# Writing out the order of all fourteen tile pairs of a fused cross-attention and sign-weight layer, and moving sums from VectorE to ScalarE

## The chip, the cores and the metric

One core of a Trainium2 chip runs the whole program. The metric is the device time in microseconds (us). The core has TensorE (PE in the profile; its weight loads are PEld), VectorE (DVE), ScalarE (ACT), GpSimd (POOL) and SyncE (SP), which here only issues DMAs.

## The reference

```python
def _layernorm(x, axis=-1, eps=1e-05):
    m = jnp.mean(x, axis=axis, keepdims=True)
    v = jnp.var(x, axis=axis, keepdims=True)
    return (x - m) / jnp.sqrt(v + eps)

# x (4, 1024, 2048), ctx (4, 64, 2048), weight (2048, 2048), bias (2048,), all float32
def xattn(query, key):
    a = jnp.einsum('bqd,bkd->bqk', query, key)
    e = jax.nn.softmax(a, axis=-1)
    return jnp.einsum('bqk,bkd->bqd', e, key)

def ffn(x, weight_real, bias):
    W = jnp.mean(jnp.abs(W), axis=1, keepdims=True) * jnp.sign(W)   # W = weight_real
    return jnp.einsum('bsi,oi->bso', x, W) + bias

x = x + jnp.tanh(g_xattn[0]) * xattn(_layernorm(x), ctx)
x = x + jnp.tanh(g_ffn[0]) * ffn(_layernorm(x), weight, bias)
```

The `ffn` lines are written here with its inner function opened.

## The kernel before, in words

The 4096 rows of x are 32 tiles of 128 rows, u = 0 to 31; each batch of 8 tiles has its own 64 keys. The work on a tile has two halves.

**Attention.** The first layer norm needs the mean and variance of the tile's rows. Tiles 0 to 2 get them on VectorE (`ln1_mean`, L1144: four `bn_stats` of 512 columns and a `bn_aggr`), the later ones on ScalarE (`sum_rows1` L730, then `square_rows1` L737, which squares x minus the mean; both write out a sum). The constant that divides them is `DVE_LN1`. GpSimd turns these into a scale and a shift of one value per row (`scale1`, `mean_1`, `rstd1`). ScalarE writes the normalised rows (`direct_high_q`, L755) and their float16 high part into `natural`, VectorE the low part (`low_q`, L1169), and a DMA transpose brings them to TensorE (`turn_q`, L411; tile 0 and tile 0 of the second norm are turned by TensorE itself). `scores(u)` (L1842) is 32 matmuls; then VectorE's `max_logits`, ScalarE's `exp`, VectorE's `split_probs` (L1215), TensorE's `transpose_probs` (L1866), ScalarE's `copy_pt` and four `attend(u, n)` (L1871), one for each 512 columns. All four write one PSUM bank, `c_ps`, so `attend(u, n + 1)` waits until VectorE's `attention(u, n)` (L1228) has added the last one to x. `attention` also takes a `bn_stats` of each chunk and a `bn_aggr` after the fourth: these are the second norm's statistics, for all 32 tiles.

**The product with the signs.** GpSimd's `scale2` (L624, four small operations) makes scale and shift, ScalarE's `normalise2` (L772) writes the normalised tile to `xn_a` or `xn_b`. Tiles 0 to 3 are multiplied plainly (`plain_block`, L1882: four quarters of 8 matmuls for each of 16 blocks). Tiles 4 to 31 go in 14 pairs p, each by a scheme of seven products instead of eight: blocks A11, A12, S3, S2, S1, A22, S4, where VectorE makes the S blocks by subtraction and addition (`make_s1` to `make_s4`). Each block goes to `natural` as a high and a low part (`high_a`, `low_a`), is turned by DMA into one of four slots of `ring_a` (`turn_a`, L420), and is multiplied in four `half_product(p, j, n, g)` (L1904) of 8 matmuls. `finish_pair` (L1254) is the VectorE work that combines, scales and adds the results to x; `store(u)` writes the tile out. A11 of pair p needs tile 2p + 5 normalised (`high_a`, L798).

**The weights.** 16 blocks of 128 rows are loaded (`load_w`), their signs written by ScalarE (`sign`, L846), the row sums of |w| taken by ScalarE (`sum_abs`, L854) or, for the blocks in `ABS_DVE` = (2, 5, 8, 11, 14), by VectorE (`sum_abs`, L1322), and the signs turned by TensorE (`turn_w`, L1824) and copied out (`take_w`). TensorE spreads the sums over columns (`turn_alpha`); a product's result is multiplied by them at the end. `make_t1`, `make_t2`, `make_t3`, `make_n4` are eight VectorE additions on the signs that the seven-product scheme needs before pair 0.

**The order of the work.** Every engine has its own program, in order, held together by semaphores. The lists are written out by hand for the start and for pairs 0 and 1. From pair 2 on each engine runs a loop over pairs with three bodies: one for pairs in `KEYS_PERIOD` (2, 6, 10: new keys arrive for the next batch), one for the pair after such a pair, and one regular. In every body f = 2p + 8 is the tile whose scores are next. Two lines of TensorE's program, with no product between them, stand at the end of the body for pairs 3, 7 and 11 (and, as `scores(11)`, at the end of pair 1):

```python
                    scores(f + 1)
                    transpose_probs(f + 1)
```

`NAT`, `REGULAR`, `SWITCH`, `AFTER` list the order in which blocks pass through the three slots of `natural`; `TURNS` the order of TensorE's own transposes.

Of the kernel before, what the change touches and what calls it, by code (L numbers as in the profile page):

```python
# [14 lines left out]
def flamingo_gated_kernel(  # L15
# [56 lines left out]
    TURNS = [("q", 0, 0), ("k", 0, 0), ("k", 0, 1), ("q", 0, 1), ("w", 0, 0), ("w", 1, 0), ("alpha", 0, 0),  # L72
              ("w", 2, 0), ("x1", 0, 0), ("w", 3, 0), ("x1", 0, 1), ("w", 4, 0), ("alpha", 1, 0), ("w", 5, 0),
# [11 lines left out]
    REGULAR = [("S1", 0, 0), ("A22", 0, 0), ("q", 0, 0), ("q", 0, 1), ("S4", 0, 0), ("A11", 1, 0), ("q", 1, 0),  # L85
               ("q", 1, 1), ("A12", 1, 0), ("S3", 1, 0), ("S2", 1, 0)]
    SWITCH = [("S1", 0, 0), ("A22", 0, 0), ("S4", 0, 0), ("q", 0, 0), ("q", 0, 1), ("A11", 1, 0), ("A12", 1, 0),
              ("S3", 1, 0), ("q", 1, 0), ("S2", 1, 0), ("q", 1, 1)]
    AFTER = [("S1", 0, 0), ("q", 0, 0), ("q", 0, 1), ("A22", 0, 0), ("S4", 0, 0), ("q", 1, 0), ("q", 1, 1),
             ("A11", 1, 0), ("S3", 1, 0), ("A12", 1, 0), ("S2", 1, 0)]  # L90
    for p in range(2, PAIRS_N):
# [27 lines left out]
    ABS_DVE = (2, 5, 8, 11, 14)  # L119
# [7 lines left out]
    def seq_y(t, n):  # L127
        return CHUNKS.index((t, n))
# [10 lines left out]
    with ExitStack() as ctx:  # L139
# [38 lines left out]
        sum1 = sb("sum1", [P, 1])  # L178
        mean1 = sb("mean1", [P, 1])
# [123 lines left out]
        mv2_set = sem("mv2_set")  # L303
        ve2_set = sem("ve2_set")
# [53 lines left out]
        DVE_LN1 = 3  # L358
# [6 lines left out]
        def _(sp):  # L365
# [74 lines left out]
            load_w(0)  # L440
            load_gates()
            load_w(1)
            load_x(1)
            load_w(2)
            load_w(3)
            load_w(4)
            load_x(2)
            load_x(3)
            turn_q(1, 0)
            load_w(5)  # L450
            turn_q(1, 1)
            load_w(7)
            load_w(6)
            turn_q(2, 0)
            turn_q(2, 1)
            load_w(8)
            load_bias()
            load_w(9)
            load_x(4)
            turn_x1(1, 0)  # L460
            turn_q(3, 0)
            turn_x1(1, 1)
            load_w(10)
            load_w(11)
            turn_q(3, 1)
            load_w(13)
            turn_x1(2, 0)
            load_w(12)
            turn_x1(2, 1)
            load_w(14)  # L470
            load_w(15)
            turn_q(4, 0)
            load_x(5)
            turn_q(4, 1)
            turn_q(5, 0)
            turn_q(5, 1)
            store(0)
            turn_x1(3, 0)
            load_x(6)
            turn_x1(3, 1)  # L480
            store(1)
            load_keys(1)
            load_x(7)
            turn_q(6, 0)
            store(2)
            turn_q(6, 1)
            load_x(8)
            turn_q(7, 0)
            turn_a(0, "A11")
            turn_q(7, 1)  # L490
            turn_a(0, "A12")
            turn_a(0, "S3")
            turn_a(0, "S2")
            turn_a(0, "S1")
            turn_a(0, "A22")
            store(3)
            turn_a(0, "S4")
            load_x(9)
            turn_q(8, 0)
            turn_q(8, 1)  # L500
            turn_keys(1)
            turn_a(1, "A11")
            store(4)
            turn_a(1, "A12")
            turn_a(1, "S3")
            load_x(10)
            turn_q(9, 0)
# [1799 lines left out]
```

## Time and profile before

| what | value |
|---|---|
| median of 3 runs | 1014.23 us (1010.57 to 1014.42) |
| the profiled execution's own time | 1012.6 us |
| its span, first to last instruction | 1010.8 us |
| busy: PE, DVE, ACT, POOL | 941.6, 870.4, 563.7, 149.8 us |
| mean granted TensorE clock | 0.981 of full speed |

The busy time of PE counts pipelined matmuls with modelled ends; where it is below a stretch's length, PE waited. The idle time of an engine matters where it is the one that sets the end.

### The profile page before, as it was taken

The page shows a single profiled execution, that of the slowest core. Times are in us where ns is not written, and L with a number is a line of the kernel's source. Part 1 is how long each engine was busy: PE and PEld are TensorE (multiplying, and loading weights), DVE is VectorE, ACT ScalarE, POOL GpSimd, SP SyncE. Part 2 cuts the span into 40 slices and gives each one's busy share as a digit, 9 for nine tenths or more (in the row PEclk, how much of TensorE's full clock was granted, in tenths as well). Part 3 has the DMA queues.
Part 4 walks back from the last instruction along what each step waited for, and adds up shares of the span by engine and source line. Part 5 has one row for each costly group of instructions (what it writes and reads, how often), then busy time and mean ns, then how long its engine had stood idle before and what let it go on. Part 6 is the DMA issues. An engine that isn't in the chain of part 4 may idle for free.

```text
span 1010.8 us, 14224 instructions
## 1 busy us (share of the span) xinstructions
PE 941.6 (93%) x5201; PEld 464.3 (46%) x5201; DVE 870.4 (86%) x1213; ACT 563.7 (56%) x617; POOL 149.8 (15%) x268
## 2 busy tenths in 40 slices
PE   2659999899999799999999899999999899999998
PEld 2435554444444344444444444444444444444443
DVE  6788999799989989897989989898989989897834
ACT  5999851545567574735557473735567473742310
POOL 0111022301112120202011120302011120302000
PEclk9779999899999899999999999999999999999999
DMA  9879718657887989796796988687797869674552
GB/s 311 270 223 240 205 22 219 178 104 170 171 198 172 226 167 227 132 201 170 164 217 121 242 172 214 143 195 173 157 215 137 239 120 214 157 162 102 112 125 83
DMA packets 365140, 178.66 MB, mean 177 GB/s; under 512 B 353424, under 2 KB 353424, under 8 KB 354448
## 3 DMA queue, kind: packets, MB, share of 16 engines
q1 hardware_dynamic: 365072, 177.76, 74.9%
q8 instruction: 41, 0.67, 0.3%
q14 instruction: 27, 0.22, 0.1%
HBM read 55.58 MB, written 33.55 MB: 88 GB/s over the span
## 4 chain that ended last, share of the span: by engine, by line
PE 56%; issue 17%; DVE 16%; POOL 4%; ACT 3%; DMA 2%; SPq 0%; POOLq 0%; ACTq 0%; DVEq 0%
PE y_ps L1930 46%; PE s_ps L1862 4%; PE c_ps L1878 4%; DVE natural L1157 3%; PE y_ps L1898 2%; DVE xr L1233 2%; DMA xr<-in_x_dram 2%; DVE xr L1365 2%; ACT xn_q L763 1%; DVE snap_a L1275 1%; DVE xr L1278 1%; DVE snap_a L1272 1%; DVE st L1236 1%; POOL nm L631 1%; POOL ve L639 1%
## 5 line engine op out<-in xcount | busy, mean ns | idle before, releaser
L1930 PE MATMUL y_ps<-wsign,ring_a 128*128 128x512 fp8e4 x1792 | 407.0, 380 | 0.0
L1930 PEld LDWEIGHTS y_ps<-wsign,ring_a 128*128 128x128 f16 x1792 | 174.4, 98 | 208.5 <-issue 2.1
L1930 PE MATMUL y_ps<-spare,ring_a 128*128 128x512 fp8e4 x896 | 198.9, 379 | 0.7 <-ACT snap_b L880 0.7
L1930 PEld LDWEIGHTS y_ps<-spare,ring_a 128*128 128x128 f16 x896 | 86.9, 98 | 105.3 <-ACT snap_b L880 1.7
L1233 DVE SCALAR_TENSOR_TENSOR xr<-c_ps,coef,xr 128x512 f32<-128x512 f32 x128 | 95.5, 746 | 26.0 <-PE c_ps L1878 25.6
L763 ACT ACTIVATE xn_q<-xr,nm,r 128x1024 f32<-128x1024 f32 x62 | 76.9, 1241 | 56.8 <-DVE natural L1157 35.4
L747 ACT ACTIVATE natural<-xn_a 128x1024 f16<-128x1024 f32 x76 | 79.2, 1053 | 44.7 <-DVE xn_a L1378 34.6
L1930 PE MATMUL y_ps<-sg,ring_a 128*128 128x512 fp8e4 x448 | 99.4, 379 | 0.0
L1157 DVE TENSOR_TENSOR natural<-xn_a,natural 128x1024 f16<-128x1024 f32 x78 | 94.7, 1216 | 4.7 <-ACT natural L747 4.7
L1878 PE MATMUL c_ps<-kd,pt 128*128 128x512 f16 x256 | 80.7, 398 | 13.8 <-DVE xr L1233 10.9
L1236 DVE BATCH_NORM_STATS2 st<-xr 128x6 f32<-128x512 f32 x128 | 88.9, 694 | 4.4
L1157 DVE TENSOR_TENSOR natural<-xn_q,natural 128x1024 f16<-128x1024 f32 x64 | 77.6, 1213 | 15.5 <-ACT natural L747 15.1
L1898 PE MATMUL y_ps<-wsign,ring_a 128*128 128x512 fp8e4 x384 | 88.5, 387 | 0.1
L1365 DVE TENSOR_TENSOR xr<-xr,bias_b 128x2048 f32<-128x2048 f32 x32 | 72.6, 2270 | 15.5 <-ACT xn_a L791 15.5
L635 POOL TENSOR_SCALAR mean<-sum 128x1 f32<-128x1 f32 x29 | 23.6, 814 | 410.2 <-ACT xn_q L735 402.6
L735 ACT ACTIVATE xn_q<-xr 128x2048 f16<-128x2048 f32 x29 | 55.4, 1910 | 26.9 <-DVE natural L1157 16.3
L741 ACT ACTIVATE xn_q<-xr,mean 128x2048 f16<-128x2048 f32 x29 | 58.0, 2001 | 20.0 <-POOL mean L635 20.0
L1862 PE MATMUL s_ps<-kt,qt 128*128 128x128 f16 x1024 | 65.3, 224 | 4.1 <-ACT qt L819 3.6
L1862 PEld LDWEIGHTS s_ps<-kt,qt 128*128 128x128 f16 x1024 | 62.7, 101 | 11.3 <-ACT qt L819 3.8
L1930 PEld LDWEIGHTS y_ps<-sg,ring_a 128*128 128x128 f16 x448 | 43.7, 98 | 52.4
L747 ACT ACTIVATE natural<-xn_q 128x1024 f16<-128x1024 f32 x62 | 65.5, 1057 | 2.0
L626 POOL TENSOR_SCALAR ve<-mv,eps 128x1 f32<-128x1 f32 x32 | 26.5, 827 | 248.8 <-DVE mv L1240 248.8
(116 smaller groups left out, 1012.3 us busy)
## 6 DMA issues: line engine op xcount, KB each, us to landing
xr<-in_x_dram SPq DMA_DIRECT2D x32, 1024.0 KB, 5.9
out_dram<-xr SPq DMA_DIRECT2D x30, 1024.0 KB, 4.6
spare<-n_L_ffn_weight_real_dram SPq DMA_DIRECT2D x8, 1024.0 KB, 6.1
ctx_f<-in_ctx_dram SPq DMA_DIRECT2D x8, 512.0 KB, 7.3
xr<-n_L_ffn_weight_real_dram SPq DMA_DIRECT2D x4, 1024.0 KB, 7.4
ctx_f<-n_L_ffn_weight_real_dram SPq DMA_DIRECT2D x4, 1024.0 KB, 6.8
out_dram<-xr SPq DMA_DIRECT2D x8, 256.0 KB, 2.2
ring_a<-natural SPq DMA_TRANSPOSE x102, 4.4
```

The source lines that it names most:

```text
L735: nc.scalar.activation(junk, xr[:, u % RX, :], ACT.Copy, accum_out=sum1[:, :]).then_inc(sum1_set, 1)
L741: nc.scalar.activation(junk, xr[:, u % RX, :], ACT.Square, bias=mean1[:, :], accum_out=sq1[:, :]).then_inc(sq1_set, 1)
L747: nc.scalar.activation(natural[:, i % RN, 0, :], src, ACT.Copy).then_inc(high_set, 1)
L763: nc.scalar.activation(xn_q[:, :], xr[:, u % RX, half(h)], ACT.Identity, bias=nm1[:, :], scale=r1[:, :]).then_inc(xn1_set, 1)
L1157: nc.vector.tensor_tensor(natural[:, i % RN, 1, :], src, natural[:, i % RN, 0, :], ALU.subtract).then_inc(low_set, 1)
L1233: nc.vector.scalar_tensor_tensor(out=xr[:, r, chunk(n)], in0=c_ps[:, :], scalar=coef[:, u % 2:u % 2 + 1], in1=xr[:, r, chunk(n)], op0=ALU. ...
L1236: nc.vector.bn_stats(st2[:, n, :], xr[:, r, chunk(n)]).then_inc(stats2, 1)
L1365: nc.vector.tensor_tensor(xr[:, r, :], xr[:, r, :], bias_b[:, :], ALU.add).then_inc(x1b_set, 1)
L1862: last = nc.tensor.matmul(s_ps[:, 0:P], qt[:, k // HALF, part, k % HALF, :], kt[:, k, :], start=(k == 0 and part == 0), stop=(k == ND - 1 ...
L1878: last = nc.tensor.matmul(c_ps[:, :], pt[:, u % 2, :], kd[:, part, chunk(n)], start=(part == 0), stop=(part == 1))
L1898: last = nc.tensor.matmul(y_ps[:, j % 4, :], x1_block(t, k // HALF)[:, part, k % HALF, :], w8[:, k // 2, chunk(n), k % 2], start=(k == 0 a ...
L1930: last = nc.tensor.matmul(y_ps[:, BANKS[j] + n, :], ring_a[:, slot_a(p, j), part, k, :], RIGHT[j][:, k // 2, chunk(n), k % 2], start=(firs ...
```

## The change

The work on VectorE and ScalarE is divided differently in three places: the sums of |w| all go to ScalarE (`ABS_DVE` is empty), the first norm's statistics of tile 2 too (`DVE_LN1` 3 to 2), and the second norm's statistics of tiles 4 to 9 (`LN2_ACT`). For these, `attention` takes a sum along with its addition in place of `bn_stats`, and ScalarE's new `square_rows2` scales and adds the four sums and squares the tile. `scale2` then has three GpSimd operations and not four.

```diff
-    ABS_DVE = (2, 5, 8, 11, 14)
+    ABS_DVE = ()
...
-        DVE_LN1 = 3
+        DVE_LN1 = 2
+        LN2_ACT = range(4,10)
...
# gpsimd, scale2(u)
+                if u in LN2_ACT:
+                    pool.wait_ge(sq2_set, sums_by(True, u) + 1)
+                    nc.gpsimd.tensor_scalar(ve2[:, :], sq2[:, :], X1_SCALE ** -2 / D, EPS * X1_SCALE ** -2, ALU.mult,
+                                            ALU.add).then_inc(ve2_set, 1)
+                    finish_scale2(u)
+                    nc.gpsimd.tensor_tensor(nm2[:, :], mean2[:, u % 2:u % 2 + 1], r2[:, :], ALU.mult).then_inc(nm2_set, 1)
+                    return
...
# scalar
+            def square_rows2(u):
+                v, m = sums_by(True, u), slice(u % 2, u % 2 + 1)
+                act.wait_ge(x1_set, (u + 1) * NC)
...
+                nc.scalar.activation(scaled2[:, :], sum2[:, u % 2, :], ACT.Copy, scale=-1.0 / D,
+                                     accum_out=mean2[:, m]).then_inc(mean2_set, 1)
+                act.wait_ge(mean2_set, v + 1)
...
+                nc.scalar.activation(junk, xr[:, u % RX, :], ACT.Square, bias=mean2[:, m],
+                                     accum_out=sq2[:, :]).then_inc(sq2_set, 1)
...
# vector, attention(u, n)
+                if u in LN2_ACT:
...
+                    nc.vector.scalar_tensor_tensor(out=xr[:, r, chunk(n)], in0=c_ps[:, :],
+                                                   scalar=coef[:, u % 2:u % 2 + 1], in1=xr[:, r, chunk(n)], op0=ALU.mult,
+                                                   op1=ALU.add, accum_out=sum2[:, u % 2, n:n + 1]).then_inc(x1_set, 1)
+                    return
```

Everything else of the change is order. The loops over pairs 2 to 13 are gone from all five programs and `NAT`; the calls of all fourteen pairs are written out one by one, in a new order also for the start and for pairs 0 and 1. No matmul, DMA or store is added or taken away. TensorE's start becomes this (before, `turn_w(1)` stood between the attends of tile 0, and four `turn_w` and two attends of tile 2 stood before the first `plain_block`; after it there are three and none):

```diff
             turn_maxima()
-            turn_rows("q", 0, 0)
             turn_keys(0)
-            turn_keys(1)
+            turn_rows("q", 0, 0)
             turn_rows("q", 0, 1)
+            turn_keys(1)
             scores(0)
             turn_w(0)
             transpose_probs(0)
             attend(0, 0)
             attend(0, 1)
-            turn_w(1)
```

and the scores of tiles 10 and 11, which stood at the end of pair 1 with their `transpose_probs` right behind, are now at these places (`...` stands for half products):

```diff
             scores(10)
+            attend(9, 3)
...
             transpose_probs(10)
-            scores(11)
-            transpose_probs(11)
...
+            attend(10, 0)
...
+            scores(11)
+            attend(10, 1)
...
+            attend(10, 2)
...
+            attend(10, 3)
+            transpose_probs(11)
...
+            attend(11, 0)
```

The same counts by tile, of half products (or plain quarters) on TensorE's list:

| between | before | after |
|---|---|---|
| `scores(u)` and `transpose_probs(u)`, u = 10 / 11 / 19 / 27 | 5 / 0 / 0 / 0 | 10 / 4 / 4 / 6 |
| the same, smallest of the other tiles from 4 on | 2 | 1 (tile 7) |
| `attend(2p + 5, 3)` and A11 of pair p, p = 0 / 1 / 2 | 8 / 11 / 6 | 13 / 12 / 10 |
| the same, pairs 3 to 13 | 18 (12 at pairs 6, 10) | 9 to 13 |

## Rows read from the trace of the kernel before

**Rows 1.** The page, part 1: busy time of each engine.
```profile
PE 941.6 (93%) x5201; PEld 464.3 (46%) x5201; DVE 870.4 (86%) x1213; ACT 563.7 (56%) x617; POOL 149.8 (15%) x268
```

**Rows 2.** Busy time by stretch; then PE clock, DMA share, GB/s.
```profile
0.00:75.78 75.78, 36.50 (x284) 26.61 (x285) 57.50 (x102) 60.49 (x61) 11.32 (x33) 0.84 0.82 268
75.78:175.00 99.22, 99.22 (x585) 50.57 (x586) 90.44 (x110) 62.41 (x61) 17.25 (x21) 1.00 0.67 170
175.00:350.00 175.00, 160.81 (x868) 77.44 (x867) 157.72 (x211) 99.66 (x110) 29.26 (x49) 0.96 0.77 174
350.00:500.00 150.00, 149.49 (x814) 72.20 (x812) 135.31 (x190) 84.99 (x96) 24.94 (x45) 1.00 0.80 177
500.00:575.00 75.00, 70.05 (x397) 34.07 (x395) 67.09 (x99) 44.68 (x53) 8.70 (x17) 1.00 0.82 193
...
725.00:800.00 75.00, 70.04 (x416) 34.85 (x414) 67.02 (x101) 42.54 (x52) 8.28 (x16) 1.00 0.83 188
```

**Rows 3.** Waits of PE from 175 to 350 us: total, times, longest.
```profile
PE s_ps L1869 <- DVE prob L1222: 9.0, 2, 7.7
PE c_ps L1878 <- DVE xr L1233: 4.3, 2, 3.2
```

**Rows 4.** Waits of PE from 350 us to the end, the same columns.
```profile
PE s_ps L1869 <- DVE prob L1222: 9.9, 6, 3.5
```

**Rows 5.** Timeline of PE around its longest wait.
```profile
335.68 0.29 PE L1869 MATMUL s_ps<-ident,prob 128*128 128x128 f16 x1 [7.71 <-DVE prob L1222]
...
336.62 4.80 PE L1930 MATMUL y_ps<-wsign,ring_a 128*128 128x512 fp8e4 x16
341.26 0.59 PE L1878 MATMUL c_ps<-kd,pt 128*128 128x512 f16 x2
```

**Rows 6.** Timeline of PE around the 3.15 us wait, three rows.
```profile
186.52 1.03 PE L1878 MATMUL c_ps<-kd,pt 128*128 128x512 f16 x2 [3.15 <-DVE xr L1233]
187.35 7.76 PE L1898 MATMUL y_ps<-wsign,ring_a 128*128 128x512 fp8e4 x24
...
195.38 5.34 PE L1898 MATMUL y_ps<-wsign,ring_a 128*128 128x512 fp8e4 x24
```

**Rows 7.** VectorE's groups over the whole span: busy, mean ns.
```profile
L1236 DVE BATCH_NORM_STATS2 st<-xr 128x6 f32<-128x512 f32 x128 | 88.9, 694 | 4.4
...
L1240 DVE BATCH_NORM_AGGREGATE mv<-st 128x2 f32<-128x24 f32 x32 | 8.4, 263 | 1.1
...
L1324 DVE TENSOR_REDUCE abs_sum<-spare 128x1 f32<-128x2048 f32 x2 | 4.5, 2274 | 0.0
...
L1302 DVE TENSOR_SCALAR lscale<-kinv 128x1 f32<-128x1 f32 x4 | 0.5, 134 | 0.0
```

**Rows 8.** ScalarE's groups from 0 to 150 us, the same columns.
```profile
L850 ACT ACTIVATE sg<-spare 128x2048 fp8e4<-128x2048 f32 x8 | 15.3, 1909 | 0.0
...
L861 ACT COPY wsign<-y_ps 128x1024 f16<-128x1024 f16 x8 | 8.0, 1001 | 2.0 <-PE y_ps L1832 2.0
...
L741 ACT ACTIVATE xn_q<-xr,mean 128x2048 f16<-128x2048 f32 x3 | 6.0, 1999 | 0.0
...
L856 ACT ACTIVATION_READ_ACCUMULATOR ctx_f<-ctx_f 128x1 f32 x3 | 0.6, 197 | 0.0
```

**Rows 9.** Busy time by stretch, from ScalarE's first work to 125 us.
```profile
10.87:125.00 114.13, 85.72 (x586) 52.11 (x587) 97.22 (x145) 103.08 (x99) 14.68 (x29) 0.90 0.85 254
```

**Rows 10.** Timeline at 124 us: the last sign block is copied out.
```profile
124.07 0.99 ACT L861 COPY wsign<-y_ps 128x1024 f16<-128x1024 f16 x1
```

**Rows 11.** Timeline: from the last tile's last chunk to its first block.
```profile
926.46 0.75 DVE L1233 SCALAR_TENSOR_TENSOR xr<-c_ps,coef,xr 128x512 f32<-128x512 f32 x1 [0.68 <-PE c_ps L1878]
...
928.34 3.22 POOL L626 TENSOR_SCALAR ve<-mv,eps 128x1 f32<-128x1 f32 x1 [8.32 <-DVE mv L1240]
...
937.98 1.22 DVE L1157 TENSOR_TENSOR natural<-xn_a,natural 128x1024 f16<-128x1024 f32 x1
```

**Rows 12.** The page, part 6: the transposes, median us from issue to landing.
```profile
ring_a<-natural SPq DMA_TRANSPOSE x102, 4.4
```

**Rows 13.** Timeline at 169.7 us: one GpSimd operation beside one of VectorE.
```profile
169.68 4.42 DVE L1398 TENSOR_TENSOR sg<-wsign,spare 128x4096 fp8e4<-128x4096 fp8e4 x1
169.89 4.25 POOL L631 TENSOR_TENSOR nm<-zero,mr 128x1 f32<-128x1 f32 x1
```

More of the change, by code:

```diff
@@ new lines, in _ @@
+            store(7)
+            turn_a(2, "S1")
+            turn_a(2, "S2")
+            load_x(13)
+            turn_q(12, 0)
+            turn_q(12, 1)
+            turn_a(2, "A22")
+            load_keys(2)
+            turn_a(2, "S4")
+            turn_q(13, 0)
+            turn_q(13, 1)
+            turn_a(3, "A11")
+            store(8)
+            turn_a(3, "A12")
+            load_x(14)
+            turn_a(3, "S3")
+            store(9)
+            turn_a(3, "S2")
+            turn_a(3, "S1")
@@ new lines, in _ @@
+            turn_a(7, "S3")
+            load_x(22)
+            store(17)
+            turn_a(7, "S2")
+            turn_a(7, "A22")
+            load_x(23)
+            turn_a(7, "S1")
+            turn_q(22, 0)
+            turn_q(22, 1)
+            turn_a(7, "S4")
+            turn_a(8, "A11")
+            turn_a(8, "A12")
+            turn_q(23, 0)
+            store(18)
+            turn_q(23, 1)
+            turn_a(8, "S3")
+            store(19)
+            load_x(24)
+            turn_a(8, "S2")
@@ L2066, in _ @@
             half_product(0, 0, 1, 1)
-            attend(6, 2)
-            scores(7)
             half_product(0, 1, 0, 0)
+            transpose_probs(6)
             half_product(0, 1, 0, 1)
+            attend(6, 0)
             half_product(0, 1, 1, 0)
@@ new lines, in _ @@
+            attend(16, 2)
+            half_product(5, 3, 0, 0)
+            transpose_probs(17)
+            half_product(5, 3, 0, 1)
+            attend(16, 3)
+            half_product(5, 3, 1, 0)
+            attend(17, 0)
+            half_product(5, 3, 1, 1)
+            attend(17, 1)
+            half_product(5, 4, 0, 0)
+            attend(17, 2)
+            half_product(5, 4, 0, 1)
+            attend(17, 3)
+            half_product(5, 4, 1, 0)
+            half_product(5, 4, 1, 1)
+            scores(18)
@@ new lines, in _ @@
+            half_product(8, 0, 0, 0)
+            attend(22, 0)
+            half_product(8, 0, 0, 1)
+            half_product(8, 0, 1, 0)
+            half_product(8, 0, 1, 1)
+            half_product(8, 1, 0, 0)
+            half_product(8, 1, 0, 1)
+            attend(22, 1)
+            scores(23)
+            half_product(8, 1, 1, 0)
+            attend(22, 2)
+            half_product(8, 1, 1, 1)
+            transpose_probs(23)
+            attend(22, 3)
+            half_product(8, 2, 0, 0)
@@ new lines, in _ @@
+            transpose_probs(25)
+            half_product(9, 3, 1, 0)
+            attend(25, 0)
+            half_product(9, 3, 1, 1)
+            attend(25, 1)
+            half_product(9, 4, 0, 0)
+            attend(25, 2)
+            half_product(9, 4, 0, 1)
+            half_product(9, 4, 1, 0)
+            attend(25, 3)
+            scores(26)
+            half_product(9, 4, 1, 1)
+            half_product(9, 5, 0, 0)
+            half_product(9, 5, 0, 1)
+            half_product(9, 5, 1, 0)
@@ new lines, in _ @@
+            transpose_probs(30)
+            half_product(12, 0, 1, 1)
+            attend(30, 0)
+            half_product(12, 1, 0, 0)
+            half_product(12, 1, 0, 1)
+            half_product(12, 1, 1, 0)
+            attend(30, 1)
+            scores(31)
+            half_product(12, 1, 1, 1)
+            half_product(12, 2, 0, 0)
+            attend(30, 2)
+            half_product(12, 2, 0, 1)
+            transpose_probs(31)
+            attend(30, 3)
+            half_product(12, 2, 1, 0)
```

2532 lines of the change are left out of this document (1700 added, 832 removed), and 30 rows, old and new, of the table NAT.

## The prediction

> **What bounds the kernel now.** I read the busy times first. PE is busy 93% of the span, DVE 86% [rows 1]: PE sets the end, and only what makes PE wait, or start late, can be won. So the second view is the table of stretches [rows 2], and in it what each stretch lacks of PE. Up to 75.78 us, where the first plain product starts, PE lacks 39.3 us, and ACT (60.5 busy) and DVE (57.5) are the busy ones. From there to 175 us PE lacks nothing. From 175 to 350 us it lacks 14.2, the two key stretches (500 to 575, 725 to 800) lack 4.95 and 4.96, and 350 to 500 lacks 0.5. The third view, PE's waits, says for what: between 175 and 350 us the transpose of the probabilities waits 9.0 us for VectorE, 7.7 of it at once, and the attends 4.3 [rows 3]; after 350 us the same transpose waits 9.9 us in six places, the longest 3.5 [rows 4]. The longest wait is that of tile 11, and the list explains it: no product stands between `scores(11)` and `transpose_probs(11)`, so PE has nothing to do through max, exp and split, and VectorE is late with these because it is full (157.7 of 175 us [rows 2]). The two waits of 3.5 us are the same place for tiles 19 and 27. A long wait also costs clock: behind the 7.71 us PE needs 4.80 us for 16 matmuls [rows 5], and behind the 3.15 us 7.76 us for 24, which later take 5.34 [rows 6].
>
> **The change, part by part**, against the profiled execution (1012.6 us, span 1010.8; the runs' median is 1.6 above it).
>
> *VectorE is relieved.* Five sums of |w| go: 5 x 2.27 = 11.4 us. Tile 2's first statistics go: 4 x 0.69 + 0.26 = 3.0. Six tiles lose four `bn_stats` and a `bn_aggr` each: 6 x (4 x 0.694 + 0.263) = 18.2 [rows 7]. Against that, 24 additions now write out a sum, and the trace has no VectorE operation that does so beside its main work. I bound the price of one from nothing (no extra work) to a `bn_stats`, 0.69, by which nothing is gained in 24 places (16.7 us). I take 0.13, VectorE's shortest operation on one value per row, because the sum is one value per row [rows 7]: 3.1 us. In all VectorE loses 32.6 - 3.1 = 29.5 us (range 16 to 33) of the 305.7 that it works before 350 us [rows 2], about a tenth, and nearly all of it before or in the stretch with 14.2 us of waits. It is worth nothing by itself: only through PE's waits.
>
> A page of the Trainium skill speaks of this price: VectorE: DVE Perf Modes, section "Two Vector instructions with no wait between them", counts an operation that also writes out its accumulator as two instructions. It gives no duration. By it the price is not nothing, and with the upper bound above the gain of 18.2 us would be 1.5; no VectorE row here shows it, though ScalarE's rows have such a second instruction of 0.197 us [rows 8].
>
> *ScalarE is loaded.* Five more sums of |w|: 5 x 2.1 = 10.5 us (a pass of 1.91, as for a sign, and 0.2 to read the sum). Two passes for tile 2: 1.9 + 2.0 + 0.4 = 4.3. Six times `square_rows2`: a pass of 2.0 and 0.2, and a four-element copy with a sum, no row of its own, between 0.2 (the shortest ScalarE row) and 0.6; 2.6 each, 15.6 in all [rows 8]. ScalarE is busy 56% of the span [rows 1] and the six lie behind 145 us, where it has room. Before 125 us it has not: 103.1 of 114.1 us [rows 9].
>
> *The start.* PE's first plain product needs `take_x1(0, 1)` on ScalarE. Ahead of that call the new list has two signs (3.8), one sum of |w| (2.1), one copy of turned signs (1.0) and one of probabilities (0.3) less, and the two passes of tile 2 (4.3) more: -2.9 us. But PE has then also done less: one `turn_w` (about 1.1 at full clock) and two attends (0.43 each) stand later, +2.0. Bounds: 0 gain to 4; I take **-1**. Tile 0's exp now stands behind the first pass of tile 2, and its copy of the probabilities behind the second; that delays its attends by some 3 us and is why I take no more.
>
> *75 to 175 us.* The last copy of turned signs ends at 125.1 us now [rows 10]. Ahead of it the new list holds seven more sums of |w| (14.7), the passes of tile 2 (4.3) and exp and copy of tile 4 (0.8): 19.8 more, so it ends at 145, with the same idle time. PE wants it before block (0, 3), nine blocks of 6.9 us and some 15 us of other work behind the first: at about 152. It fits. But inside, at the fifth and sixth `turn_w`, my count of ScalarE's passes comes out within 1 us of PE's arrival, so ScalarE's 11 us of idle time [rows 9] may come back as PE's. Bounds 0 to 8; I take **+2**.
>
> *175 to 350 us.* Tile 11 gets four half products of 1.7 us between its scores and the transpose, tile 10 ten instead of five. VectorE comes with 29 us less in hand. The 9.0 us go, and of the attends' 4.3 I leave 2: -11.3. The clock's loss goes with the long waits: (7.76 - 5.34) + (4.80 - 3.62, what 16 matmuls take unhindered) = 3.6. Together **-14.9**; bounds -3 (the waits move to the attends) and -17.8 (all).
>
> *Key stretches.* Tiles 19 and 27 get four and six half products where none stood: 2 x 3.5 goes, the remaining 2.9 stay. **-7**; bounds 0 and -11.6 (with the 1.7 us of single waits elsewhere). VectorE's load is not changed there: 67.1 of 75 us [rows 2], and the 7.9 us idle have to be used better.
>
> *The pairs' feed.* From pair 3 on, the new list leaves 9 to 13 half products between the last attend of a tile and A11 of its pair, where mostly 18 stood. Nine are 15.6 us, with the scores or attends among them 17.4. How long is that way? For the last tile from 926.46 to the end of the low part at 939.20 [rows 11], plus 4.4 for the transpose [rows 12]: 17.1 us. That is with 3.2 us in a GpSimd operation that takes 0.27 when free. So at seven pairs (2, 3, 4, 6, 10, 12, 13, with 9 or 10) the feed is just in time. Bounds 0 and the rival below; I take one miss of 3: **+3**.
>
> What holds GpSimd is seen in [rows 13]: an operation on one value per row takes 4.25 us beside a 4.42 us VectorE operation with two SBUF inputs. The Trainium skill, SBUF — State Buffer, section "Who interferes with whom", says the same and more: such a VectorE instruction keeps a GpSimd instruction that reads SBUF out for its whole length. By that rule each of the three GpSimd operations left in the way of tiles 4 to 9 can lose a 1.2 us subtraction; the sum would carry up to 3.7 us more at a pair that has no slack. The trace agrees with it where it can be seen.
>
> *Nothing for the rest.* Matmuls and DMAs are the same. The lists of `natural` and the DMA order only follow. The last pair's 69 us of products run alone at full clock, and two VectorE operations and a store follow them, as now.
>
> Sum: -1 + 2 - 14.9 - 7 + 3 = -17.9, so 994.7 for the profiled execution and **996** for the median.
>
> **Rivals.**
> 1. *All waits go*: -1, 0, -17.8, -11.6, 0: 982 (profiled), 984 by the median. For it: VectorE's relief lies right ahead of the waits. Against: lists with so little slack never run without a miss.
> 2. *ScalarE bounds the start*: the 75 to 175 us term is +8 and the clock falls with it (2.4, as in [rows 6]): 996 + 8.4 = 1004. For: 103 of 114 us busy, and 20 us more to do. Against: the sums of |w| stand late in the list.
> 3. *The waits only move* (this is also the case where the change does not do what it says, because a written-out sum costs VectorE as much as a `bn_stats`): the softmax is no longer waited for, but the attends are, since `c_ps` is one bank. The terms are -1, +2, -3, -2, +1: 1011. For: VectorE at 90% throughout. Against: before 350 us at least 14 us of its work are surely gone.
> 4. *Slower: the feed comes too late.* Place: A11 of the seven pairs with 9 or 10 half products. If the way takes 22.5 us instead of 17.1 (one subtraction, one bias addition of 2.3 us and a late transpose ahead of it), each misses by about 5: +35 in place of +3, 996 + 32 = 1028. It decides from 17.4 + 20.9 / 7 = 20.4 us on, where it eats the whole gain. For: the way was measured with VectorE nearly free, and mid-kernel it is 90% full. Against: VectorE's list has been written anew as well, and pair 2 now has 6 half products and no wait of A11 shows.
>
> **How the numbers follow.** My forecast has 0.52, rival 1 0.10, rival 2 0.12, rival 3 0.14, rival 4 0.12. A difference under 0.5% (5 us) can't be told from none here. Faster: forecast and rivals 1 and 2 (0.74) and 0.04 of rival 3, 0.78. Same: 0.09 of rival 3. Slower: rival 4 and the last 0.01 of rival 3, 0.13. The range takes rivals 1 to 3: from 981 to 1013; what it leaves out is rival 4 and the tails.
>
> **What would show it.** Right: no wait of the transpose over 2 us for tiles 11, 19, 27; PE short by under 4 us between 175 and 350; VectorE's busy time near 841; a first plain product at 73 to 75 us; ScalarE's at about 594. Wrong: waits of PE for a block in `ring_a` or a DMA (rival 4), for `wsign` on ScalarE before 150 us (rival 2), for `xr` in many places (rival 3), or an extra VectorE group beside the additions with more than 0.3 us each.

## The result, and the profile after

The changed kernel takes **986.13 us** (median of 4 runs, 984.6 to 986.62), the kernel before in the same job 1014.33 (4 runs, 1010.57 to 1014.46): a ratio of 0.9729, 95% interval [0.9712, 0.9747], or 28 us less. That is inside the forecast range and 10 us below the forecast itself. The profiled execution took 985.79 us, with a span of 984.0, against 1012.6 and 1010.8.

The page of the changed kernel, part 1, answers to [rows 1]:

```profile
PE 934.0 (95%) x5201; PEld 462.9 (47%) x5201; DVE 840.8 (85%) x1197; ACT 589.3 (60%) x655; POOL 134.9 (14%) x262
```

VectorE loses 29.6 us (forecast 29.5), ScalarE gains 25.6 (forecast 30.4). PE's busy time falls by 7.6 us though its 5201 matmuls are the same: the mean granted clock is 0.988 instead of 0.981. The stretches, with the columns of [rows 2]:

```profile
0.00:71.61 71.61, 33.14 (x264) 24.17 (x265) 47.32 (x89) 57.72 (x60) 8.05 (x33) 0.83 0.76 250
75.00:175.00 100.00, 99.36 (x600) 51.08 (x598) 81.85 (x111) 77.29 (x77) 14.52 (x19) 1.00 0.71 193
175.00:350.00 175.00, 172.50 (x945) 83.84 (x944) 154.24 (x218) 119.22 (x140) 28.12 (x49) 1.00 0.82 181
350.00:500.00 150.00, 148.80 (x810) 72.00 (x809) 137.73 (x193) 86.52 (x97) 21.14 (x41) 1.00 0.87 186
500.00:575.00 75.00, 73.75 (x415) 36.10 (x413) 66.08 (x98) 42.40 (x52) 11.80 (x23) 1.00 0.83 190
575.00:725.00 150.00, 148.56 (x810) 72.09 (x811) 137.47 (x195) 87.97 (x99) 21.95 (x42) 1.00 0.81 178
725.00:800.00 75.00, 74.67 (x420) 36.77 (x419) 67.79 (x101) 42.91 (x51) 12.41 (x23) 1.00 0.83 185
```

The stretch from 175 to 350 us lacks 2.5 us of PE where it lacked 14.2, and its clock is 1.00 where it was 0.96; the two key stretches lack 1.25 and 0.33 where they lacked 4.95 and 4.96. The first plain product starts at 71.61 us instead of 75.78. What PE still waits for behind it, all of it, with the columns of [rows 3]:

```profile
PE c_ps L2569 <- DVE xr L1656: 2.9, 3, 1.6
PE y_ps L2621 <- DMA ring_a<-natural: 1.5, 1, 1.5
PE y_ps L2621 <- DVE snap_a L1689: 0.8, 2, 0.6
PE y_ps L2621 <- ACT snap_b L1087: 0.7, 1, 0.7
PE y_ps L2530 <- DVE snap_b L1762: 0.6, 1, 0.6
PE y_ps L2589 <- DVE ring_a L1616: 0.6, 1, 0.6
PE c_ps L2569 <- ACT pt L1043: 0.3, 1, 0.3
PE s_ps L2560 <- DVE prob L1636: 0.3, 1, 0.3
```

The wait for the probabilities, 9.0 us in [rows 3] and 9.9 in [rows 4], is 0.3 us. That looks like the forecast's story. For the waits of the transpose it is; for the rest, and for what VectorE's relief is worth, the experiments tell another one.

### The profile page after: what moved, and what is told of

The parts are those of the page before. It is cut to its first block, busy times and chain, and to the rows that moved or that the text cites. A ratio compares the mean times of both kernels' runs of the same rounds, so it can differ in the third digit from the quotient of the medians.

```text
span 984.0 us, 14349 instructions
## 1 busy us (share of the span) xinstructions
PE 934.0 (95%) x5201; PEld 462.9 (47%) x5201; DVE 840.8 (85%) x1197; ACT 589.3 (60%) x655; POOL 134.9 (14%) x262
## 4 chain that ended last, share of the span: by engine, by line
PE 69%; DVE 10%; issue 7%; ACT 5%; POOL 2%; DMA 2%; SPq 0%; ACTq 0%; DVEq 0%; POOLq 0%
PE y_ps L2621 53%; PE y_ps L2589 7%; PE c_ps L2569 5%; PE s_ps L2553 4%; DVE natural L1571 3%; ACT xn_q L952 1%; DVE xr L1656 1%; DMA xr<-in_x_dram 1%; ACT natural L933 1%; DMA ring_a<-natural 1%; ACT spare L1063 1%; DVE st L1661 1%; DVE snap_a L1689 0%; ACT xn_q L919 0%; DVE xr L1790 0%
## 5 line engine op out<-in xcount | busy, mean ns | idle before, releaser
L2621 PE MATMUL y_ps<-wsign,ring_a 128*128 128x512 fp8e4 x1792 | 400.6, 379 | 2.3 <-DMA ring_a<-natural 1.5
L2621 PE MATMUL y_ps<-spare,ring_a 128*128 128x512 fp8e4 x896 | 202.8, 379 | 0.7 <-ACT snap_b L1087 0.7
L1656 DVE SCALAR_TENSOR_TENSOR xr<-c_ps,coef,xr 128x512 f32<-128x512 f32 x104 | 77.6, 746 | 21.5 <-PE c_ps L2569 21.1
L2569 PE MATMUL c_ps<-kd,pt 128*128 128x512 f16 x256 | 79.7, 394 | 11.5 <-DVE xr L1656 8.6
L2589 PE MATMUL y_ps<-wsign,ring_a 128*128 128x512 fp8e4 x384 | 85.2, 379 | 0.6 <-DVE ring_a L1616 0.6
L1661 DVE BATCH_NORM_STATS2 st<-xr 128x6 f32<-128x512 f32 x104 | 72.2, 694 | 3.6
L784 POOL TENSOR_SCALAR mean<-sum 128x1 f32<-128x1 f32 x30 | 14.7, 489 | 415.9 <-ACT xn_q L919 398.8
L919 ACT ACTIVATE xn_q<-xr 128x2048 f16<-128x2048 f32 x30 | 57.2, 1907 | 17.4 <-DMA xr<-in_x_dram 12.0
L1703 DVE TENSOR_TENSOR xr<-snap_a,xr 128x512 f32<-128x512 f32 x84 | 58.1, 692 | 2.9
```

Of the source, the lines that this page charges most:

```text
L1656: nc.vector.scalar_tensor_tensor(out=xr[:, r, chunk(n)], in0=c_ps[:, :], scalar=coef[:, u % 2:u % 2 + 1], in1=xr[:, r, chunk(n)], op0=ALU. ...
L1661: nc.vector.bn_stats(st2[:, n, :], xr[:, r, chunk(n)]).then_inc(stats2, 1)
L1703: nc.vector.tensor_tensor(xr[:, r, chunk(m)], tmp, xr[:, r, chunk(m)], ALU.add).then_inc(y_added, 1)
L2569: last = nc.tensor.matmul(c_ps[:, :], pt[:, u % 2, :], kd[:, part, chunk(n)], start=(part == 0), stop=(part == 1))
L2589: last = nc.tensor.matmul(y_ps[:, j % 4, :], x1_block(t, k // HALF)[:, part, k % HALF, :], w8[:, k // 2, chunk(n), k % 2], start=(k == 0 a ...
L2621: last = nc.tensor.matmul(y_ps[:, BANKS[j] + n, :], ring_a[:, slot_a(p, j), part, k, :], RIGHT[j][:, k // 2, chunk(n), k % 2], start=(firs ...
```

## The experiments

Medians in us; each ratio is against the kernel before on the same chip. The kernel before took 1012.97 in the first job (order_alone to before_ln2), 1012.33 in the second (after_abs_back to feed_after) and 1013.82 in the third.

**order_alone: the new order without the shifts.** The three shifts of work to ScalarE are taken back (their calls leave ScalarE's and GpSimd's lists, `sum_abs` and `ln1_mean(2)` come back into VectorE's), the rewritten lists stay. Where VectorE's five sums and tile 2's statistics stand in the new list is my choice, here and below.

```
-        ABS_DVE = ()
+        ABS_DVE = (2, 5, 8, 11, 14)
-        DVE_LN1 = 2
+        DVE_LN1 = 3
-        LN2_ACT = range(4, 10)
+        LN2_ACT = ()
```

> The changed kernel's order in every program, but all three shifts of work taken back: VectorE again sums |w| of five blocks, takes tile 2's first statistics and all second-norm statistics. If the order is what counts, it stays within 4 us of the change (986 to 990). If VectorE's relief is what removes the wait of 7.7 us and those around it, much of the 14 us between 175 and 350 us comes back: 998 to 1005. My own theory takes both as needed: about 995, the waits returning as waits of the attends for VectorE between 175 and 350 us.

Measured: 1000.05 (998.64 to 1001.41), ratio 0.9869 [0.9852, 0.9885]. Its stretches:

```profile
75.00:175.00 100.00, 90.60 (x523) 45.69 (x522) 83.42 (x104) 66.38 (x62) 11.05 (x20) 0.97 0.63 165
175.00:350.00 175.00, 171.52 (x961) 83.72 (x960) 163.18 (x216) 98.56 (x111) 27.77 (x46) 1.00 0.80 185
```

The order alone gives 13 us. From 175 to 350 us it removes 10.7 of the 14.2 us, although VectorE is busier than before (163.2 us; 157.7 in [rows 2]). So most of the waits there did not need a relieved VectorE. In exchange PE lacks 9.4 us between 75 and 175, where before it lacked nothing.

**shifts_alone: the old order with the shifts.** All three shifts in the old lists; `square_rows2(6)` stands ahead of `direct_high_q(8, 0)`, and those of 7 to 9 ahead of `normalise2` of the same tile, as that of 5.

```
-        ABS_DVE = (2, 5, 8, 11, 14)
+        ABS_DVE = ()
-        DVE_LN1 = 3
+        DVE_LN1 = 2
+        LN2_ACT = range(4, 10)
+            square_rows2(4)
             sum_rows1(6)
 ...
+            square_rows2(5)
             normalise2(5)
```

> The old order with all three shifts of work to ScalarE. If relief counts, 995 to 1000. If the order counts, over 1005, with the wait of tile 11's probabilities only shortened, since no product stands between its scores and its transpose: a softmax chain of about 2.5 us is bare in any case at tiles 11, 19 and 27. My theory: 1002, the 7.7 us wait down to about 3, the two of 3.5 us unchanged, because VectorE does the same work there.

Measured: 1041.1 (1037.55 to 1042.08), ratio 1.0262 [1.0238, 1.0287]. PE's largest wait from 20 us to the end:

```profile
PE s_ps L1935 <- DVE prob L1283: 40.6, 13, 8.1
```

28 us slower, with VectorE's work smaller by the same 29 us (841.5 busy). The direction is the one expected if the order counts, but my own theory was 39 us lower. The parts don't add: -13 and +28 apart, -28 together. The placement of the ScalarE calls is mine, and ScalarE's queue stands still at each until the tile's last attend is done; another placement may lose less.

**before_ln2: the old order with the second norm's shift alone.** The same placement of `square_rows2`, and nothing else of it.

```
+        LN2_ACT = range(4, 10)
```

> The kernel before with only the second-norm statistics of tiles 4 to 9 moved to ScalarE. VectorE has 16 us less before the wait of 7.7 us at 335 us. If that wait is VectorE's backlog, it falls to the bare softmax chain of 2.5 us and the small ones before it go too: 1003 to 1006. If it is the missing product between scores and transpose alone, nothing changes: 1012 to 1015.

Measured: 1026.84 (1026.32 to 1027.48), ratio 1.0134 [1.0119, 1.0149].

```profile
175.00:350.00 175.00, 149.76 (x808) 72.69 (x806) 130.70 (x190) 102.62 (x120) 18.00 (x41) 0.93 0.70 155
```

Again slower than every expectation. VectorE is busy 130.7 of the 175 us instead of 157.7, and PE lacks 25.2 us instead of 14.2. Part of the smaller busy time is only that less got done (808 matmuls, not 868). The statistics' way through ScalarE (a copy, a pass of 2.0 us, behind whatever stands in its queue) made everything later: in this stretch VectorE waits 32.4 us for ScalarE's high parts, where it waited 8.3. So the run shows that this relief costs more than it gives in the old order. It doesn't show what a relief without a new delay would do.

**after_ln2_back: the change without the second norm's shift.** The six `square_rows2` leave ScalarE's list.

```
-        LN2_ACT = range(4, 10)
+        LN2_ACT = ()
```

> The change with only the second-norm statistics of tiles 4 to 9 back on VectorE (24 bn_stats and 6 bn_aggr, 18.2 us of VectorE's time, between 110 and 320 us). By my sum this relief is part of 11 us; with the new order the rest of VectorE's idle time can take most of it: I expect 988 to 991. A rival, that VectorE bounds the stretch from 125 to 350 us, gives 986 + 16 = 1002.

Measured: 987.25 (986.77 to 987.92), ratio 0.9743 [0.9729, 0.9758], 1.1 us above the change's 986.13, with intervals of the ratio that overlap. The part that gives VectorE 18.2 of its 29.5 us is worth about one us, if anything.

```profile
175.00:350.00 175.00, 171.51 (x938) 82.67 (x936) 165.03 (x220) 106.33 (x120) 31.42 (x54) 1.00 0.81 181
```

VectorE is 94% busy there, and PE lacks one us more than in the change.

**after_abs_back: the change with the five sums of |w| on VectorE again.** `sum_abs(5)` stands behind `low_q(2, 1)`, (8) behind `take_w(4)`, (11) behind `take_w(5)`, (14) behind `spread_alpha(11)`.

```
-        ABS_DVE = ()
+        ABS_DVE = (2, 5, 8, 11, 14)
             take_keys(1)
+            sum_abs(2)
```

> The change with only the five sums of |w| back on VectorE, each ahead of the operation that it stood ahead of before. The order alone lost 9.4 us of TensorE between 75 and 175 us, 7.0 of it before one transpose of spread sums. If these sums are the cause, this kernel has most of that loss: 993 to 998. If tile 2's statistics are, it stays at 986 to 988.

Measured: 995.18 (993.58 to 996.95), ratio 0.9821 [0.9801, 0.9841]: 9 us of the change. Its trace has them at the start and in one stretch:

```profile
75.00:175.00 100.00, 94.14 (x564) 48.00 (x563) 82.98 (x105) 67.99 (x65) 10.21 (x19) 0.98 0.67 177
```

PE lacks 5.9 us where the change lacks 0.6, and the first plain product starts 1.9 us later, at 73.54. Here five sums of 2.27 us stand in VectorE's queue ahead of copies and additions that PE waits for. This is the shift that counts, and it counts in the stretch in which I had put a loss.

**after_ln1_back: tile 2's first statistics on VectorE again.** Its two passes leave ScalarE's list, its mean GpSimd's.

```
-        DVE_LN1 = 2
+        DVE_LN1 = 3
             gate_scale(0)
+            ln1_mean(2)
```

> The change with only tile 2's first statistics back on VectorE, between the gate scale and the maximum of tile 0. Theory: they delay tile 0's softmax by 3 us on VectorE but free ScalarE of 4.3 us ahead of its exp; within 2 us of the change. Rival, that the start is bound by VectorE: 3 us or more slower, the first plain product at 74 us or later.

Measured: 986.31 (984.54 to 987.92), ratio 0.9732 [0.9712, 0.9753]. No difference from the change. The three shifts taken back one at a time cost 9, 1 and 0 us, all together (order_alone) 14; the other 4 appear only when they are taken back together.

**before_gap: the kernel before with products in the gap.** The forecast held that tiles 11, 19 and 27 wait 7.7, 3.5 and 3.5 us because no product stands between their scores and their transpose. This edit puts four half products there, and nothing else.

```
             transpose_probs(10)
             scores(11)
-            transpose_probs(11)
 ...
                     scores(f + 1)
-                    transpose_probs(f + 1)
 ...
                     half_product(p, 0, 1, 1)
+                    if p - 2 in KEYS_PERIOD:
+                        transpose_probs(f - 1)
```

> The kernel before with one edit: the transpose of the probabilities of tiles 11, 19 and 27 stands four half products later, in the next pair. If the missing products are the cause of the waits of 7.7, 3.5 and 3.5 us, up to 14 us go: 1000 to 1005. If VectorE's backlog is, the wait moves to the attends, since VectorE adds tile 10's first chunk only after tile 11's split: 1009 to 1014. My theory: the two of 3.5 us go mostly, the 7.7 us becomes some 4 at an attend: 1005.

Measured: 1027.23 (1023.89 to 1031.49), ratio 1.0141 [1.0102, 1.018]: 15 us slower, and slower than every expectation. PE's waits from 175 to 350 us, and from 350 us to the end:

```profile
PE c_ps L1878 <- DVE xr L1233: 7.6, 3, 3.3
PE y_ps L1930 <- DVE snap_a L1264: 5.1, 1, 5.1
PE s_ps L1869 <- DVE prob L1222: 1.3, 1, 1.3
...
PE c_ps L1878 <- DVE xr L1233: 13.0, 9, 3.3
PE s_ps L1869 <- DVE prob L1222: 3.0, 4, 1.0
```

The wait of the transpose goes from 18.9 us to 4.3, as the gap's theory says. But the attends wait 20.6 us instead of 5, and a bank 5.1. A transposed block of probabilities is copied by ScalarE, in order, and ScalarE now stands at that copy:

```profile
342.94 0.27 ACT L836 COPY pt<-s_ps 128x128 f16<-128x128 f16 x1 [7.52 <-PE s_ps L1869]
```

7.5 us idle, and what stands behind the copy starts late: the high part of `xn_b` 6.7 us later than in the kernel before (343.11 us, not 336.40), though the stretch up to there ran 0.9 us ahead. So filling the gap by itself doesn't pay. It doesn't show that the gap was not the cause of the wait: the lists of ScalarE and VectorE stayed as they were, and a run that moves ScalarE's copy along with the transpose was not made.

The traces of the kernel before and of the change say more. Tile 11 before: the scores, a bias addition, the maximum, the end of exp, the split.

```profile
326.02 1.95 PE L1862 MATMUL s_ps<-kt,qt 128*128 128x128 f16 x32 [0.50 <-ACT pt L836]
327.54 2.29 DVE L1365 TENSOR_TENSOR xr<-xr,bias_b 128x2048 f32<-128x2048 f32 x1
329.75 0.28 DVE L1207 TENSOR_REDUCE logits<-s_ps 128x64 f32<-128x128 f32 x1
330.92 0.18 ACT L829 ACTIVATION_READ_ACCUMULATOR ex<-logits,neg_max,lscale 128x1 f32 x1
335.40 0.23 DVE L1222 SCALAR_TENSOR_TENSOR prob<-ex,prob 128x64 f16<-128x64 f32 x1
```

The split ends 7.7 us behind the scores. 1.8 of it the maximum stands behind a bias addition, and 4.1 (331.10 to 335.18) the split stands behind five other operations of VectorE's list. At tiles where nothing stands between (9, 13), the whole way takes 2.3 us. Now tile 11 in the change, and tile 19 before and in the change (scores, split, transpose):

```profile
326.19 1.95 PE L2553 MATMUL s_ps<-kt,qt 128*128 128x128 f16 x32
333.89 0.23 DVE L1636 SCALAR_TENSOR_TENSOR prob<-ex,prob 128x64 f16<-128x64 f32 x1
336.18 0.22 PE L2560 MATMUL s_ps<-ident,prob 128*128 128x128 f16 x1
```

```profile
560.48 1.95 PE L1862 MATMUL s_ps<-kt,qt 128*128 128x128 f16 x32
565.59 0.22 DVE L1222 SCALAR_TENSOR_TENSOR prob<-ex,prob 128x64 f16<-128x64 f32 x1
```

```profile
545.03 1.95 PE L2553 MATMUL s_ps<-kt,qt 128*128 128x128 f16 x32
552.17 0.23 DVE L1636 SCALAR_TENSOR_TENSOR prob<-ex,prob 128x64 f16<-128x64 f32 x1
554.59 0.22 PE L2560 MATMUL s_ps<-ident,prob 128*128 128x128 f16 x1
```

In the change the split ends 6.0 us behind the scores at tile 11 (7.7 before), 5.4 at tile 19 (3.4 before) and 5.5 at tile 27 (3.4 before). It is hardly earlier at the first and later at the other two. PE doesn't wait for it because it has 8.0, 7.6 and 11.9 us of products and attends there. So the waits of the transpose go because the gap is filled, in a list where the other engines' calls move with it.

**feed_after: 3.6 us more on the feed's way, in the change.** What I had called the feed is: last attend of a tile, its statistics, GpSimd's scale, ScalarE's normalisation, VectorE's low part, transpose, A11. For tiles 10 to 31, 14 small writes stand ahead of GpSimd's scale, for both tiles of a pair; nobody reads what they write by then.

```
                 pool.wait_ge(mv2_set, ...)
+                if u >= 10:
+                    pool.wait_ge(alpha_tr, NC)
+                    for k in range(14):
+                        nc.gpsimd.memset(ident[:, :], 0.0).then_inc(pad_set, 1)
+                        pool.wait_ge(pad_set, 14 * (u - 10) + k + 1)
```

> The change with 14 small memsets ahead of GpSimd's scale of each tile from 10 on, some 4 us more on the way from the last attend to the pair's first block. By the rival of the prediction the way takes 17 us where 17.4 are free, so it costs about 4 us at each of six pairs: 1005 to 1012. If the new order has shortened the way, since no bias addition stands in it any more (8.3 us from the last chunk to the low part at the last pair, where it was 12.7), it is hidden: under 990.

Measured: 1018.83 (1014.48 to 1021.61), ratio 1.0052 [1.0023, 1.0081], 32.7 us above the change and more than was expected. The 14 take 3.61 us, and eleven pairs have them.

```profile
PE y_ps L2627 <- DVE snap_a L1695: 19.9, 9, 4.4
```

**feed_small: the same with 4 writes, about 1.0 us.**

> The change with 4 memsets (1.0 us) there. With 3.6 us costing 33 us over 11 pairs, 3 us a pair, a way without any slack would lose 1.0 x 11 = 11 us: 997. If there are 1 to 2 us of slack at most pairs: 987 to 990.

Measured: 997.67 (996.27 to 998.44), ratio 0.9845 [0.9824, 0.9866], 11.5 us above the change.

```profile
PE y_ps L2627 <- DVE snap_a L1695: 8.4, 5, 3.6
```

1.0 us in eleven pairs costs 11.5 us; 3.6 us in eleven pairs, 39.7 in all, cost 32.7. There is no slack at all: a us on this way, at both tiles of a pair, costs about one us per pair from the first. The wait is not seen at the block that comes late (`ring_a`) but at a PSUM bank (`y_ps` for `snap_a`): VectorE stands in order at the low part, and behind it stand the additions of `finish_pair` that free the banks. From 350 us to the end VectorE waits 23.7 us for ScalarE's high parts in the change, 34.2 in feed_small and 53.6 in feed_after. GpSimd's other work stands behind the writes too, such as the first norm's mean of a later tile; these runs don't separate that share.

**feed_before: the 14 writes in the kernel before.**

> The kernel before with the same 14 memsets (3.6 us) ahead of GpSimd's scale of each tile from 10 on, which cost the change 33 us. If the old order's 18 half products between last attend and A11 are slack, it loses little: 1013 to 1018. If GpSimd's way is critical in either order, because the wait goes over VectorE's queue and not over A11 itself, it loses as much as the change did: 1035 to 1048. My guess is in between, 1025.

Measured: 1066.0 (1064.63 to 1067.21), ratio 1.0525 [1.0499, 1.0551]: +52 us, 4.7 per pair for 3.6.

```profile
PE y_ps L1936 <- ACT snap_b L886: 24.7, 7, 4.2
```

More than any expectation. Where 18 half products stand between last attend and A11 there is no slack either, so half products in PE's list were the wrong thing to count. The bank is freed by ScalarE here, not by VectorE: its copy stands in order behind a normalisation that waits for GpSimd's scale (3.0 us just ahead of PE's wait of 4.2). The cost above the delay's own length is in PE's busy time. In the profiled executions the 5201 matmuls take 960.9 us instead of 941.6, at a mean granted clock of 0.958 instead of 0.981. Of the 52 us that is 19.3, and PE's waits are 32.7, or 3.0 per pair.

**bias_early: the bias additions back ahead of A11.** `add_bias` is 2.3 us of VectorE. The old list has the second tile's ahead of `low_a(p, "A11")` in seven of the pairs 3 to 13, and the first tile's in all eleven, mostly right behind its pair's last attend. The new one has the second tile's behind it in all eleven, the first tile's in seven. This edit puts both ahead in all eleven, so it moves 18 additions.

```
             attention(2p + 5, 3)
+            add_bias(2p + 4)
 ...
+            add_bias(2p + 5)
             low_a(p, "A11")
 ...
-            add_bias(2p + 4), add_bias(2p + 5)
```

> The change with one part of the old order: from pair 3 on both bias additions of a pair (2.3 us each on VectorE) stand again ahead of the low part of A11, the first right behind the tile's last attention. They are then in the way that the memsets lengthened, by up to 4.6 us at once and by what GpSimd waits for them. If that way decides: over 1005. If VectorE's queue has the time: 986 to 992.

Measured: 1018.61 (1009.52 to 1020.97), ratio 1.0042 [1.0018, 1.0066]. 32.5 us, the whole gain and a little more, for the same work in another place. Waits from 175 us on, and the quiet stretch of [rows 2]:

```profile
PE y_ps L2621 <- DVE snap_a L1689: 17.4, 11, 3.5
```

```profile
350.00:500.00 150.00, 141.78 (x762) 68.04 (x761) 131.67 (x183) 77.84 (x86) 24.61 (x40) 0.98 0.76 168
```

The wait is at the same bank as in the two feed runs, eleven times now, and the stretch that lacked 1.2 us lacks 8.2. The way to it is a shorter one: VectorE waits for ScalarE's high parts no longer than in the change (23.6 us from 350 us on, 23.7 there), so what comes late to the banks is, as it seems, VectorE's list itself, behind its own additions. 8.5 of the 29.3 us between the profiled executions are PE's busy time (942.5 against 934.0).

The run shows what the new order needs, not what it gained. The old order has most of these additions ahead of A11 too, and from 350 us on PE's named waits there come to 11.6 us in all. In its regular pairs, with both additions ahead, PE lacks only 0.5 of 150 us. And the edit starts at pair 3: from 175 to 350 us PE is busy 173.3 us in this run and 172.5 in the change. The old order with its additions moved back was not run.

**lean_scale: a shorter way.** For the tiles whose statistics VectorE takes, GpSimd's last two operations become one.

```
-                nc.gpsimd.tensor_tensor(mr2[:, :], mv2[:, 0:1], r2[:, :], ALU.mult).then_inc(mr2_set, 1)
-                pool.wait_ge(mr2_set, sums_by(False, u) + 1)
-                nc.gpsimd.tensor_tensor(nm2[:, :], zero[:, :], mr2[:, :], ALU.subtract).then_inc(nm2_set, 1)
+                nc.gpsimd.tensor_scalar(nm2[:, :], mv2[:, 0:1], r2[:, 0:1], -1.0, ALU.mult, ALU.mult).then_inc(nm2_set, 1)
```

> A candidate that could beat both: the change with the last two of GpSimd's four operations of a tile with VectorE's statistics made one (shift = mean x scale x -1), for 26 tiles. The way loses 0.2 us, and up to 0.7 where GpSimd waits for VectorE. TensorE waits only 7 us behind its start: 983 to 986.5. Nothing (986) if the order has slack everywhere now.

Measured: 985.32 (983.25 to 985.86), ratio 0.9721 [0.9699, 0.9742]. 0.8 us below the change, and the intervals overlap: not shown to be faster. A us more per tile costs eleven, but a few tenths of a us less give next to nothing, so something else seems to be next in line at once.

## Why the prediction was right or wrong

One correction to what stands ahead of it: key blocks are made in pairs 0, 4 and 8, and the scores with no product before their transpose stand at the end of the bodies of pairs 1, 5 and 9. The tiles (11, 19, 27) and the rows are as given there.

**The start (forecast -1).** 4.2 us earlier, with 20 matmuls less done by then (264 against 284), the 2.0 us that the forecast counted: -2.2 in effect. The first plain product came earlier than the 73 to 75 us of the forecast. Right in kind; but 1.9 us of it go in after_abs_back, so much of it is VectorE's relief, which the forecast didn't count there, and not ScalarE's list alone.

**75 to 175 us (forecast +2).** PE lacks 0.6. The sum was nearly right, and its working was not: I had looked only at what ScalarE takes on, never at what VectorE gives up there. Against the same order without the shift it is a gain of 5 us in this stretch. ScalarE was not the bound (rival 2 did not come).

**175 to 350 us (forecast -14.9).** Measured: 11.7 us less of waits, and with the forecast's 3.6 of clock (which is 1.00 and was 0.96) -15.3. Right in size, and right in the first step of the cause: "no product stands between" holds for the transpose, as tiles 11, 19 and 27 of the change show. Filling the gap was not enough by itself (before_gap). The second step was wrong. "VectorE is late because it is full" doesn't hold in the new order: VectorE is 93 and 94% busy in order_alone and after_ln2_back, and PE lacks 3.5 us in either. What the traces show in its place is the order of VectorE's list: 5.9 of tile 11's 7.7 us are other operations ahead of the maximum and the split. How the attends' 4.3 us and the small rest went is not taken apart. The bias additions from pair 3 on have no part in this stretch.

**Key stretches (forecast -7).** -8.3, for the reason that the forecast gave: the split of tiles 19 and 27 comes 2 us later than before, and products cover it.

**The feed (forecast +3).** The step that failed most. A delay on the feed's way does cost PE time, as rival 4 has it and the feed runs show (11.5 and 32.7 us), but by another mechanism: PE waits for a bank and not for a block in `ring_a`. By my count a way of 12.8 us (below) against 17.4 would leave 4.6 us free, and there are none. And the misses didn't come (the one wait of PE for a DMA transpose, 1.5 us at 261 us, is ahead of pair 3), since I had measured the length of the way on the kernel before and carried it over whole. That way had two bias additions in it, which the change takes out. The last pair's before, in rows that I had read only by their ends [rows 11]:

```profile
928.15 2.23 DVE L1365 TENSOR_TENSOR xr<-xr,bias_b 128x2048 f32<-128x2048 f32 x1
...
930.30 1.21 DVE L1157 TENSOR_TENSOR natural<-xn_a,natural 128x1024 f16<-128x1024 f32 x1
...
935.77 2.29 DVE L1365 TENSOR_TENSOR xr<-xr,bias_b 128x2048 f32<-128x2048 f32 x1 [2.21 <-ACT xn_a L791]
```

The first addition is not in VectorE's way, but it and the subtraction behind it hold GpSimd's one-value operation of [rows 11] until 931.56, when the subtraction (931.51) is over. The second stands in front of the low part. After:

```profile
914.65 0.74 DVE L1656 SCALAR_TENSOR_TENSOR xr<-c_ps,coef,xr 128x512 f32<-128x512 f32 x1
...
916.53 0.27 POOL L775 TENSOR_SCALAR ve<-mv,eps 128x1 f32<-128x1 f32 x1 [11.21 <-DVE mv L1665]
...
918.50 2.09 ACT L998 ACTIVATE xn_a<-xr,nm,r 128x2048 f32<-128x2048 f32 x1 [4.38 <-POOL nm L780]
...
921.72 1.23 DVE L1571 TENSOR_TENSOR natural<-xn_a,natural 128x1024 f16<-128x1024 f32 x1 [1.24 <-ACT natural L933]
...
926.04 2.29 DVE L1790 TENSOR_TENSOR xr<-xr,bias_b 128x2048 f32<-128x2048 f32 x1
```

8.30 us from 914.65 to 922.95, where it was 12.74 from 926.46 to 939.20, and the addition follows at 926.04. With 4.5 for the transpose it is 12.8 us, not 17.1. The 3.22 us operation takes 0.27. The Trainium skill, SBUF — State Buffer, section "Who interferes with whom", has the rule (VectorE's second pair of ports is GpSimd's, one at a time), and both timelines agree with it. I had used it only to add to the price of the change, not to ask what the new order takes away from beside GpSimd's operations.

**VectorE's and ScalarE's busy time.** 840.8 against "near 841", 589.3 against 594. The price of a written-out sum, of which I took 0.13 us, is 0.08:

```profile
L1651 DVE DVE_READ_ACCUMULATOR xr<-c_ps,coef,xr 128x1 f32 x24 | 2.0, 82 | 0.0
L1651 DVE SCALAR_TENSOR_TENSOR xr<-c_ps,coef,xr 128x512 f32<-128x512 f32 x24 | 17.9, 747 | 8.6 <-PE c_ps L2569 8.4
L1656 DVE SCALAR_TENSOR_TENSOR xr<-c_ps,coef,xr 128x512 f32<-128x512 f32 x104 | 77.6, 746 | 21.5 <-PE c_ps L2569 21.1
```

It is a second instruction, as the Trainium skill counts it (VectorE: DVE Perf Modes, "Two Vector instructions with no wait between them"), and the addition itself is no longer than without it (747 and 746 ns).

**The rivals.** Rival 1 (984, all waits go) is nearest to what was measured, 986.1; I had held it unlikely, since lists with so little slack miss now and then. They have no slack on the way, as the feed runs show, and still miss only 7.7 us in 912. Rival 3 (the waits only move) is what happens, and with a loss, when the gap is filled by itself. Rival 4's price, by another way, is what happens when the bias additions stand in the wrong place of the new lists.

**The sum.** -2.2 + 0.6 - 15.3 - 8.3 of these terms; the regular stretches (350 to 500 and 575 to 725) lack 2.6 us instead of 1.0, +1.6 (waits for attends and for a bank; the one wait for a DMA transpose, 1.5, lies in the stretch from 175 to 350 us); 800 to 950 us lacked 0.7 and lacks nothing. That is -24.3 of the -26.8 between the profiled executions. The other 2.5 us are in PE's busy time, which falls by more than the named clock losses. 0.9 of them are the two pairs of attend matmuls right behind the two long waits, 1.03 us [rows 6] and 1.04 where such a pair otherwise takes 0.59; the remaining 1.6 stay open. Open too: what each call moved in the lists before pair 3 is worth by itself, and how much of the 13 us of the order alone is the bias additions (behind 350 us it can't be more than the waits there, 11.6 us, and the clock that they cost).

## What to carry to other kernels

When several in-order engines feed each other, write down the way of one tile through the slowest chain of small operations, and look in each queue for the long operations that stand ahead of it; in the changed kernel 18 additions of 2.3 us in the wrong place cost 32 us, and 18 us less work on a 90% busy engine gave about one. Measure slack instead of counting it: put a known delay into the way (1 us, then 4) and see whether the time moves. When you fill an empty spot in one engine's list, move the other engines' calls with it, or the wait comes back elsewhere. Measure a way's length again, or take it apart operation by operation, when the change touches what stands in it.

## What was unexpected of the hardware

A GpSimd operation on one value per row has no fixed price: it depends on what VectorE's list puts beside it. The same `ve` operation of the second norm means, in the kernel before, in the change and in bias_early (busy us, mean ns, idle before it):

```profile
L626 POOL TENSOR_SCALAR ve<-mv,eps 128x1 f32<-128x1 f32 x32 | 26.5, 827 | 248.8 <-DVE mv L1240 248.8
```

```profile
L775 POOL TENSOR_SCALAR ve<-mv,eps 128x1 f32<-128x1 f32 x26 | 16.5, 635 | 197.4 <-DVE mv L1665 197.4
```

```profile
L775 POOL TENSOR_SCALAR ve<-mv,eps 128x1 f32<-128x1 f32 x26 | 26.7, 1026 | 208.1 <-DVE mv L1665 208.1
```

827, 635 and 1026 ns, with the shortest at 0.26 us. GpSimd is 14 or 15% busy in all of them, so its share of the span says little of what it costs.

And a delay can cost more than its length: 3.6 us on the way of each pair cost 4.7 per pair in the old order, and 3.0 in the new. In the old order 1.8 of the 4.7 are PE's longer busy time at the lower granted clock (19.3 us in eleven pairs), in the new 0.8 (943.3 against 934.0 us). bias_early also scatters more (11.5 us between its ten runs) than the change (2.0 between four).
